# Four of the first eight token loads issued from ScalarE's DMA queue instead of SyncE's

## The reference

```python
x = x + 0.5 * ffn(layernorm(x), w_gate, w_up, w_down)
x = x + scan_layer(layernorm(x), W, lam_logit, eta, gamma, beta)
x = x + 0.5 * ffn(layernorm(x), w_gate, w_up, w_down)
# ffn:        (silu(x @ w_gate.T) * (x @ w_up.T)) @ w_down.T, hidden size 2048
# scan_layer: z = x @ W.T; m_k[t] = sigmoid(lam_logit)[k] * m_k[t-1] + z[t], k = 0..3
#             h = z + sum_k eta[k] * m_k; gamma * layernorm(h) + beta
```

## Time and profile before

| | |
|---|---|
| median of 3 runs | 1054.81 us (1054.34 to 1056.26) |
| profiled execution | 1055.73 us, of which the span of the trace is 1053.9 us |
| PE busy | 1045.9 us (99%) |
| DVE, ACT, POOL busy | 642.2 us (61%), 352.3 us (33%), 107.2 us (10%) |
| granted TensorE clock, mean | 0.998 |
| chain that ended last | PE 97%, DMA 1%, DVE 1% |
| DMA | 215.80 MB, mean 205 GB/s |

### The profile page before, as it was taken

How to read it: one execution, slowest core, us unless ns; L and a number is a source line. 1 busy time by engine, 2 the same in 40 slices (tenths; PEclk the granted TensorE clock), 3 DMA queues, 4 the chain that set the end, 5 groups by cost and what they waited for, 6 DMA issues and landing times.

```text
span 1053.9 us, 12828 instructions
## 1 busy us (share of the span) xinstructions
PE 1045.9 (99%) x4742; PEld 866.7 (82%) x4742; DVE 642.2 (61%) x973; ACT 352.3 (33%) x589; POOL 107.2 (10%) x127
## 2 busy tenths in 40 slices
PE   9999999999999999999999999999999999999998
PEld 8888888878888888888888888888888888888887
DVE  6855666557777657877757865687665333333342
ACT  6644544524322232222522223222233322222321
POOL 3123332110020110001002001000000000000000
PEclk9999999999999999999999999999999999999999
DMA  6588866765655555656546555555566566556265
GB/s 200 216 321 311 311 249 247 269 235 188 230 188 184 183 178 202 206 181 198 173 141 213 190 179 180 183 197 180 194 206 219 191 194 200 184 185 199 86 215 184
DMA packets 56845, 215.80 MB, mean 205 GB/s; under 512 B 5840, under 2 KB 15056, under 8 KB 48848
## 3 DMA queue, kind: packets, MB, share of 16 engines
q1 hardware_dynamic: 56640, 214.98, 60.0%
q10 hardware_dynamic: 144, 0.00, 0.0%
HBM read 170.92 MB, written 44.04 MB: 204 GB/s over the span
## 4 chain that ended last, share of the span: by engine, by line
PE 97%; DMA 1%; DVE 1%; DVEq 0%; issue 0%; SPq 0%
PE ps_a L1294 8%; PE ps_a L1296 8%; PE ps_a L1295 8%; PE ps_b L1296 8%; PE ps_b L1295 8%; PE ps_b L1294 8%; PE ps_c L1294 6%; PE ps_c L1296 6%; PE ps_c L1295 6%; PE ps_d L1296 6%; PE ps_d L1294 6%; PE ps_d L1295 6%; PE aux L1296 3%; PE aux L1294 3%; PE aux L1295 3%; PE ps_d L1494 1%
## 5 line engine op out<-in xcount | busy, mean ns | idle before, releaser
L844 DVE TENSOR_TENSOR tmp<-tmp,ps_c 128x512 f32<-128x512 f32 x59 | 40.5, 687 | 139.1 <-PE ps_c L1296 139.1
L1294 PE MATMUL ps_a<-xt,gu 128*128 128x512 f32 x304 | 119.5, 393 | 0.0
L1296 PE MATMUL ps_a<-xt,gu 128*128 128x512 f32 x304 | 118.4, 390 | 0.0
L1295 PE MATMUL ps_a<-xt,gu 128*128 128x512 f32 x304 | 118.3, 389 | 0.0
L1294 PE MATMUL ps_b<-xt,gu 128*128 128x512 f32 x286 | 111.8, 391 | 0.0
L1296 PE MATMUL ps_b<-xt,gu 128*128 128x512 f32 x286 | 111.4, 389 | 0.0
L1295 PE MATMUL ps_b<-xt,gu 128*128 128x512 f32 x286 | 111.3, 389 | 0.0
L1294 PE MATMUL ps_d<-dn,hid 128*128 128x512 f32 x256 | 100.8, 394 | 0.0
L1296 PE MATMUL ps_d<-dn,hid 128*128 128x512 f32 x256 | 99.8, 390 | 0.0
L1295 PE MATMUL ps_d<-dn,hid 128*128 128x512 f32 x256 | 99.7, 389 | 0.0
L1294 PE MATMUL ps_c<-xt,gu 128*128 128x512 f32 x236 | 92.1, 390 | 0.0
(11 more groups left out here) (204 smaller groups left out, 2035.5 us busy)
## 6 DMA issues: line engine op xcount, KB each, us to landing
dn<-dn_kept SPq DMA_DIRECT2D x112, 512.0 KB, 3.2
gu<-gu_kept SPq DMA_DIRECT2D x46, 1024.0 KB, 5.0
gu<-gu_kept SPq DMA_DIRECT2D x46, 768.0 KB, 5.4
gu_kept<-gu SPq DMA_DIRECT2D x16, 1024.0 KB, 4.5
gu_kept<-gu SPq DMA_DIRECT2D x16, 768.0 KB, 4.2
dn_kept<-dn SPq DMA_DIRECT2D x16, 512.0 KB, 5.1
zw<-zw_kept SPq DMA_DIRECT2D x16, 512.0 KB, 3.2
h_t<-w_ffn_in SPq DMA_DIRECT2D x18, 256.0 KB, 4.8
```

The lines of the kernel that those rows point to most:

```text
L844: dve.tensor_tensor(dst, u3s(si), p5_bank(si)[:, :], ALU.add).then_inc(c22_done, 1)
L1294: pe.matmul(dst, a_hi, b_hi, start=start, stop=False, skip_group_check=chained)
L1295: pe.matmul(dst, a_hi, b_lo, start=False, stop=False, skip_group_check=chained)
L1296: return pe.matmul(dst, a_lo, b_hi, start=False, stop=stop, skip_group_check=chained)
```

## The change

ScalarE issues units 1, 3, 5 and 7, ahead of its `lam_logit` load. SyncE issues units 0 and 2, both loads of stage 0, units 4 and 6, and then as before.

```diff
-            for r in range(4):
+            for r in (0, 2):
                 load_x_unit(r)
             load_stage(0)
-            for r in range(4, 8):
+            for r in (4, 6):
                 load_x_unit(r)
             load_stage(1)
             load_stage(2)
@@ ScalarE's list
+            x_v = x_in.rearrange("b (s p) d -> b p s d", p=P)
+            for r in (1, 3, 5, 7):
+                act.dma_start(x_tok[:, r, :], x_v[r // ST, :, r % ST, :]).then_inc(x_unit[r], 16)
             act.dma_start(lam_tmp[:, 0, :], lam_logit_in.rearrange("(o k) -> o k", o=1).to_broadcast([P, K])
                           ).then_inc(lam_arrived, 16)
             act.wait_ge(lam_arrived, 16)
```

## The result

| | before | after |
|---|---|---|
| median | 1056.11 us (7 runs, 1054.34 to 1056.5) | 1059.37 us (7 runs, 1058.2 to 1061.62) |
| profiled execution: time, span | 1055.73, 1053.9 us | 1059.37, 1057.6 us |
| first plain product starts | 12.71 us | 14.52 us |

The ratio is 1.0035 with a 95% interval of 1.0025 to 1.0045: slower beyond its interval, by 3.3 us between the two medians and by 3.7 us by the ratio. Two executions, one of 6066.85 us of the kernel before and one of 2735.24 us of the two-queue run with 19 unread products, were in a slow state and are left out everywhere.

A forecast was written before the change was run, and what follows sets the result against it. TensorE was taken to bound nearly all, its first product set by token load and ScalarE. A late lam_logit adds 1.8 us, swallowing the 0.3 us token gain: 1054.81 becomes 1056.6 us, range 1054.9 to 1059.1.

The forecast's parts named there:

- What bounds the head: Kernel start: ScalarE waits for lam_logit, landing at 9.9 us instead of 5.13, so the first product comes 1.8 us later.
- rival 3: Head: queues share by bytes (lam_logit at 10.6 us) or it lands behind everything (11.9); loss 2.5 to 3.8 us; chance 0.09.
- the 7 that were to show it: Sign in the profile after: ScalarE idle about 7 us ahead of its exponential instead of 2.73, released by the lam_logit load.
- Rival 1: Before the first plain product: TensorE's clock falls in the new 1.8 us gap, costing 1.4 us more, 1058.0 us; chance 0.18.
- The token term: VectorE's first statistics: unit 1 lands earlier, gain taken as 0.3 us, at most 0.38, lost in the wait for ScalarE.
- The sum: Whole kernel: the head's +1.8 us added to the median of 1054.81 us gives 1056.6 us.

The follow-up runs named there:

- two-queue run with 19 unread products: Changed kernel with the lam_logit load taken out of the head and 19 unread TensorE products at the start instead of 22; ratio 0.9983.
- gap-filled kernel: Changed kernel with 11 instead of 5 unread TensorE products after unit 3; ratio 1.0024, median 1058.98 us.
- late one-queue run: Kernel before, all token units on SyncE's queue, with SyncE issuing the lam_logit load behind unit 6; ratio 1.0044.

## Why the prediction was wrong

The changed kernel took 1059.37 us, 2.8 us more than the forecast of 1056.6. Of these 1.3 us are the base, and 1.5 us are the clock and the last phase; the loss at the head was right.

- **What bounds the head, right in its mechanism, with luck in its number.** The `lam_logit` load was forecast to land at 9.9 us and landed at 10.27; from landing to the fourth `hi_first` 4.4 us were forecast and 4.2 measured; the first product was forecast at 14.5 us and came at 14.52. The forecast of +1.8 us was the head's loss to within 0.1 us, in both profiles of the changed kernel (14.52, 14.62). But the landing came out of three wrong terms that cancel. Ahead of the small load passed eight transfers, not seven (the count of rival 3, +0.7 us); the engines were full from about 3.5 us instead of 4.98, so the eight were through at 8.0 instead of 10.2 us (-2.2); and the small pieces took 2.3 us instead of 0.4 (+1.9). Added up, that is 9.9 + 0.7 - 2.2 + 1.9 = 10.3. ScalarE's idle time was 5.62 us, not the 7 that were to show it, because its table load now stands behind the issues, at 3.39 us.
- **The clock, the step that failed.** Rival 1 was given 0.18, because its idle time of 1.8 us is shorter than the 2.51 us that had brought the clock down. But the gap was not 1.8: it was 1.85 in one profile and 2.62 in the other, since the earlier tokens let TensorE finish its turns sooner while the end of the gap stayed. I had written that the token gain "disappears into the wait for ScalarE"; it lengthened the idle time. The fall was priced at 1.4 us and measured at 1.7. Seven of twelve executions had a mean clock under 0.998, where before three of 92 had. The length of the idle time does not settle it alone: 1.85 and 2.00 us left the clock where it was, 2.62 and 3.39 us brought it down, and the stall of 2.5 us at 216 us did either.
- **The last phase, not foreseen.** "Behind the first product all engines are shifted alike" is true of engines and not of transfers: in the first profile 1.56 us were lost behind the output store, and moving that store takes 1.4 us off the gap-filled kernel. Between executions of the changed kernel this comes and goes, and why is open.
- **The token term, mis-sized.** Its upper bound was 0.38 us; measured were 6.67 - 5.71 = 0.96. The bound held unit 0 at its old landing. But up to 4.98 us the engines were slow because the small pieces ran there, and with these moved back unit 0 landed at 0.74 + 3.7 = 4.44 us. I had read 4.4 and 4.2 us to landing as two loads that do not disturb each other; both were slow.
- **The base.** The sum was put on the median of three runs, 1054.81 us; seven gave 1056.11, of a kernel whose spans differ by 1.6 us with the clock behind one stall. On that base +1.8 is 1057.9 us, still 1.5 short, and that is the clock and the last phase.

## What to carry to other kernels

Before DMA issues are put on a compute engine's queue, look at what stands behind them there: a wait on a tiny load becomes a wait on everything ahead of it in that queue, and it holds the whole engine. Move such a load, and its wait, out of the head first; here that and three unread products fewer started the first product 1.16 us earlier with one queue, as early as two queues did. In time that was 0.1%, with an interval that reaches 1.0000. When the start of a kernel bound by TensorE is delayed, price the idle time in front of it as well as the delay: a fall of the clock can cost as much again.

## What the runs showed of the hardware

A 2 KB load in 16-byte pieces slows all other traffic while it passes. The engines moved 117 GB/s from 8 to 9 us in the changed kernel and 104 GB/s from 6 to 7 us with two units on ScalarE, with other loads queued in both, against 372 to 406 GB/s in the full stretches around. The dip moved with that load. Without it, in the two-queue run with 19 unread products, no half microsecond from 3.5 to 13.5 us is below 344 GB/s. With one queue and no such load in the head the rate is less even, but its lowest half microsecond from 2.5 to 13.5 us is 201 GB/s.

```profile
5.00:6.00 1.00, 1.00 (x7) 1.00 (x7) 0.89 (x5) 0.00 (x0) 0.00 (x0) 1.00 0.73 242
6.00:7.00 1.00, 1.00 (x9) 1.00 (x9) 1.00 (x3) 0.00 (x0) 0.70 (x1) 1.00 0.43 104
```

(Stretches of the kernel with two units on ScalarE, columns as above.)

In the kernel before the same pass lay in the first 5 us and looked like the slow start of the DMA engines; without it, in the late one-queue run, units 0 and 1 were there by 3.55 us.

The same stall of 2.5 us, behind down weights at 216 us, left the clock at 1.00 in one execution of the kernel before and brought it to 0.50 in another; their spans are 1052.6 and 1053.9 us. Any comparison of a few microseconds on this kernel has to match the clock or take many runs.
